# A graph attention loop whose first six steps of rows are gathered in the preparation, with later gathers of the first round not held back

## The chip, the cores and the metric

The kernel runs on one core of a Trainium2 chip. The metric is the device time of one execution in microseconds (us). The engines are named as in the profile: PE (matmul) and PEld (its weight load), DVE, ACT, POOL and SP. POOL issues the indirect DMAs ("gathers"), SP issues the ordinary ones.

## The reference, cut to what matters

One layer has three parts: a GATv2 graph attention, a four-layer linear-attention mixer over all 3125 nodes, and a mixture of eight experts. The change touches the first part only. There the graph has 3125 nodes with 256 features, 100,000 edges sorted by destination, and 4 heads of 64.

```python
x_l = (x @ W_l.T + b_l).reshape(n, HEADS, DIMS)
x_r = (x @ W_r.T + b_r).reshape(n, HEADS, DIMS)
...
s = x_l[src] + x_r[dst] + e_feat
s = jax.nn.leaky_relu(s, NEG_SLOPE)
alpha = jnp.einsum('ehc,hc->eh', s, att)
...
alpha = ex / (denom[dst] + 1e-16)
out = jax.ops.segment_sum(alpha[..., None] * x_l[src], dst, num_segments=n)
```

`x_l[src]` is the gather: each edge needs the row of its source node.

## The kernel before

The graph attention runs in three blocks, one after the other, and all engines meet at the end of each: the preparation (normalise, the products with W_l and W_r, index tables), the edge loop, and a closing block. Then come the mixer and the experts.

**Tiles and steps.** Edges are cut in items of 128 (TE). A step takes four items (IG), so it needs four gathers of 128 rows with 264 numbers each (GD) out of `xl_d`, the array of left products in the chip's main memory. There are 210 steps, in 15 rounds of 14 (RING). Round 0 is written out, rounds 1 to 14 are a loop (`rounds`, L1350 on), and its head is pinned to a fixed slot of a fetch block (`head_slot`), so that code ahead of it does not shift its body. The rows of a step lie in one of 14 places: the first six in `zone` (called XS in the profile), which in the preparation held x, the other eight in `ring` (called a_g).

**A step.** For step t of a round:

- SP loads, two steps ahead, the local destinations `DB` (a_db, L1399), and four steps ahead the edge attributes (a_lt, L1403). At step 5 it also stores two staged arrays of 448 KB each (L1433, L1434).
- DVE makes the one-hot matrix of the next step (L1642), then takes leaky relu times attention in two halves (`gate`, L1652), then sums per head (L1731). One L1731 ends each step of scores.
- PE computes the scores of items 0 and 1 (L1505, and L1506 that adds the gathered rows), counted by the semaphore a_scored0; then those of items 2 and 3 (L1512), counted by a_scored1, for which ACT has copied the gathered rows into PSUM (L1596).
- Ten to twelve steps later ACT weighs the rows (L1614), PE sums them (L1519) and DVE adds them up (L1659). From t = 7 of round 0 there is also a running maximum over batches of seven steps, the "chain".

PE's instructions for a step stand in the order first scores, chain, second scores, sums, and each engine runs its own list in order.

**Who waits for the rows.** The semaphore a_g of step t counts 16 for each gather that has landed. POOL issues the gathers of a step when the scores of three steps before are done (AHEAD = 3): it waits for a_scored0 ahead of the first of the four and for a_scored1 ahead of the third. Before step 2 of each round, POOL also gathers two staged arrays (L1471). In round 0 the first four steps (EARLY = 4) are an exception. The preparation gathers their 16 x 128 rows into `zone` (L1086), POOL waits for all of them at the end of the preparation (semaphore g_early), and the readers on PE (L1528) and ACT (L1593) do not wait in the loop.

**The end of the preparation.** DVE compares neighbouring edges' keys (L1284 to L1292), SP stores the result, two times 448 KB (L994), and a last small array (L996), and waits for these to land. Then the engines meet.

Of the kernel before, what the change touches and what calls it, by code (L numbers as in the profile page):

```python
# [36 lines left out]
IG = 4  # L37
# [11 lines left out]
RI = IG * RING  # L49
STAGED = RI * (ROUNDS + 2)  # L50
ZSLOTS = NT * D // (IG * GD)
EARLY = 4
LTS = BSTEPS
EA0 = GD
MW = EA0 + ED + 1
# [809 lines left out]
def graph_attention(nc, s, zone, XS, ident, x, xn_d, g, sums_d, scratch, ln1, ln1_of, scale0):  # L865
# [9 lines left out]
    with ExitStack() as keep:  # L875
# [4 lines left out]
        SRCX = kept("g_srcx", [TE, ITEMS], I32)  # L880
# [7 lines left out]
        with ExitStack() as c:  # L888
# [146 lines left out]
            def _(p):  # L1035
# [48 lines left out]
                p.wait_ge(s["p_xl_d"], 16 * (NW // XW))  # L1084
                for n in range(IG * EARLY):
                    p.indirect_dma_start(out=zone[:, n * GD:(n + 1) * GD], out_offset=None, in_=xl_d,  # L1086
                                         in_offset=bass.IndirectOffsetOnAxis(ap=SRCX[:, n:n + 1], axis=0)).then_inc(s["g_early"], 16)
                p.wait_ge(s["g_early"], 16 * IG * EARLY)

            @block.tensor  # L1090
            def _(pe):
# [210 lines left out]
        with ExitStack() as mid:  # L1302
# [3 lines left out]
            with ExitStack() as c:  # L1306
# [64 lines left out]
                def at_start(i):  # L1371

                    return isinstance(i, int) and i == 0

                def rows_landed(i, t):

                    return 64 * i if t < EARLY else 64 * i + 64

                def chain_of(i, t):

# [80 lines left out]
                def _(p):  # L1461
# [3 lines left out]
                    def slot(i, base, t):  # L1465
                        if t == GATHER_AT:
                            p.wait_ge(s["s_tiles"], 16 * i + 16)
                            wait(p, "s_staged", 32 * i, 0)
                            p.sem_inc(s["a_seen"], 1)
                            for n, a in enumerate((g["eaT"], g["ea"])):  # L1470
                                p.indirect_dma_start(out=STG[:, n, :], out_offset=None, in_=a,  # L1471
                                                     in_offset=bass.IndirectOffsetOnAxis(ap=TIX[:, 0:1], axis=0)).then_inc(s["s_gathered"], 16)
                        if t % BSTEPS == 0:
                            p.wait_ge(s[f"a_ix{t // BSTEPS}"], 16 * i + 16)
                            p.sem_inc(s["a_seen"], 1)
                        if at_start(i) and t < EARLY:
                            return
                        wait(p, "b_weighed", base, t + 1 - RING)
                        p.sem_inc(s["a_seen"], 1)
                        for j in range(IG):  # L1480
                            n = IG * (t % BSTEPS) + j
                            if j % 2 == 0:
                                wait(p, f"a_scored{j // 2}", base, t + 1 - AHEAD)
                                p.sem_inc(s["a_seen"], 1)
                            p.indirect_dma_start(out=gathered(t)[:, j, :], out_offset=None, in_=xl_d,  # L1485
                                                 in_offset=bass.IndirectOffsetOnAxis(ap=IX[:, t // BSTEPS, n:n + 1], axis=0)).then_inc(s[f"a_g{t}"], 16)
# [4 lines left out]
                def _(pe):  # L1491
                    def slot(i, base, t):
# [29 lines left out]
                        if scoring:  # L1522
# [2 lines left out]
                            ws = [pe.snap(both & 31).with_bounds(min_val=0, max_val=NW - 1), pe.snap(both >> 5).with_bounds(min_val=0, max_val=NW - 1)]  # L1525
                            wait(pe, "a_onehot", base, t + 1)
                            pe.wait_ge(s[f"a_eat{t % LTS}"], 32 * i + 16 * (t // LTS) + 16)
                            if not (at_start(i) and t < EARLY):  # L1528
                                pe.wait_ge(s[f"a_g{t}"], rows_landed(i, t))
                            scores_of_first(ws)  # L1530

                        if tau == 0:
# [55 lines left out]
                def _(a):  # L1588
                    def slot(i, base, t):
                        tau, odd, n = chain_of(i, t)  # L1590
                        par = 1 if odd else 0
                        if exists(base, t, 0):
                            if not (at_start(i) and t < EARLY):  # L1593
                                a.wait_ge(s[f"a_g{t}"], rows_landed(i, t))
                            wait(a, "a_gated1", base, t)
                            a.activation(pS[0:TE, 2:4, 0:GD], gathered(t)[:, 2:4, :], ACT.Copy).then_inc(s["a_filled"], 1)  # L1596
                        if tau == 3:
# [1010 lines left out]
```

## Time and profile before

| | us |
|---|---|
| median of 3 runs | 3437.3 |
| lowest, highest run | 3428.2, 3441.15 |
| the profiled execution | 3411.32 |
| its span (first to last instruction) | 3409.5 |
| mean granted TensorE clock | 0.953 |

The span is what the trace covers; about 2 us lie around it. The page gives busy times over the whole span: PE 3021.3 us (89%), DVE 1829.7 (54%), ACT 1508.7 (44%), POOL 1195.2 (35%). In the trace the preparation ends and the edge loop's block begins between 108 and 109 us. The edge loop ends at about 1543 us. The rest is the closing block, the mixer and the experts. A share over the whole says little of round 0, which lies between 109 and about 190 us. For that the timeline rows below are read.

### The profile page before, as it was taken

How to read it: one execution, taken by the hardware profiler on the slowest of the kernel's cores; microseconds unless marked ns; L12 is line 12 of the kernel's file. 1: busy time of each engine (PE TensorE's matmuls, PEld its weight loads, DVE VectorE, ACT ScalarE, POOL GpSimd, SP SyncE). 2: the span in 40 equal slices, each digit the busy share in tenths (PEclk: the TensorE clock that was granted, in tenths of full speed). 3: DMA queues.
4: the chain of work that ended last, by engine and by line, in shares of the span. 5: the costliest groups of instructions: out<-in, count | busy, mean ns of one | idle time of the engine just before them, and what ended most of it. 6: DMA issues, size and time to landing. Idle time of an engine off the chain costs nothing. (4 is left out here: it accounts for less than half of the span.)

```text
span 3409.5 us, 50817 instructions
## 1 busy us (share of the span) xinstructions
PE 3021.3 (89%) x13612; PEld 2391.3 (70%) x13613; DVE 1829.7 (54%) x3640; ACT 1508.7 (44%) x4942; POOL 1195.2 (35%) x1153
## 2 busy tenths in 40 slices
PE   6688888888888888884999999999999999999999
PEld 4456566556665556653778877877777888888898
DVE  5566676677666666676854464374455435111103
ACT  2067677677667667675422322232231222222232
POOL 4565565665656656530320041030012000222210
PEclk9798898999899998997999999999999999999999
DMA  7566665665666656543211011000001014333361
GB/s 216 151 152 146 149 143 141 150 150 144 149 148 149 148 146 144 143 97 116 63 38 37 27 31 31 27 22 1 15 27 50 1 39 162 120 120 120 121 173 41
DMA packets 288782, 345.06 MB, mean 101 GB/s; under 512 B 155205, under 2 KB 213684, under 8 KB 284666
## 3 DMA queue, kind: packets, MB, share of 16 engines
q1 hardware_dynamic: 232813, 174.79, 19.4%
q0 software_dynamic: 53632, 157.89, 18.0%
q10 hardware_dynamic: 2218, 10.81, 1.0%
q8 instruction: 74, 1.21, 0.2%
q14 instruction: 45, 0.37, 0.0%
HBM read 298.03 MB, written 44.37 MB: 100 GB/s over the span
## 5 line engine op out<-in xcount | busy, mean ns | idle before, releaser
L1485 POOL DMA_INDIRECT a_g<-xl_d,a_ix x480 | 475.0, 990 | 285.5 <-issue 124.5
L1519 PE MATMUL b_pM<-b_m,b_oh 128*112 128x281 f32 x1680 | 501.5, 443 | 44.5 <-DVE g_acc L1659 38.1
L1614 ACT ACTIVATE b_m<-a_g,c_pcx 128x64 f32<-128x64 f32 x1856 | 457.3, 333 | 13.1 <-issue 13.1
L1519 PEld LDWEIGHTS b_pM<-b_m,b_oh 128*112 128x112 f32 x1680 | 317.5, 195 | 174.9 <-issue 90.9
L1485 POOL DMA_INDIRECT XS<-xl_d,a_ix x344 | 337.0, 980 | 208.7 <-issue 92.5
L1652 DVE SCALAR_TENSOR_TENSOR a_r<-a_pS,g_attx 128x528 f32<-128x528 f32 x420 | 287.4, 700 | 192.2 <-remote 109.4
L1614 ACT ACTIVATE b_m<-XS,c_pcx 128x64 f32<-128x64 f32 x1424 | 349.3, 333 | 3.2 <-issue 3.2
L2306 ACT ACTIVATE f_hid<-f_pH,f_b 128x256 f32<-128x256 f32 (+3 forms) x360 | 162.0, 452 | 424.7 <-PE f_pH L2189 415.6
L449 PE MATMUL m_pH<-m_h,m_w 128*128 128x313 f32 (+1 forms) x1280 | 342.3, 426 | 4.5 <-DVE m_h L629 4.5
L125 POOL TENSOR_TENSOR m_rstd<-m_ve,m_mhalf 125x5 f32<-125x5 f32 x40 | 46.9, 1172 | 769.3 <-DVE m_ve L111 769.3
L449 PEld LDWEIGHTS m_pH<-m_h,m_w 128*128 128x128 f32 x1280 | 241.3, 189 | 97.2 <-issue 5.3
L1505 PE MATMUL a_pS<-g_xr,a_lt 128*128 x840 | 278.0, 414 | 20.7 <-issue 14.6
L1512 PE MATMUL a_pS<-g_xr,a_lt 128*128 x840 | 236.4, 405 | 65.0 <-ACT a_pS L1596 28.0
L2211 PE MATMUL f_pO<-f_w,f_hid 128*128 (+1 forms) x1296 | 287.3, 379 | 1.3 <-DVE XS L2443 1.3
L605 ACT ACTIVATE m_hid<-m_pH,m_b 128x313 f32<-128x313 f32 x320 | 149.5, 519 | 276.4 <-PE m_pH L449 276.4
L2211 PEld LDWEIGHTS f_pO<-f_w,f_hid 128*128 128x128 f32 (+1 forms) x1296 | 242.4, 189 | 34.2 <-ACT f_hid L2306 1.7
L1731 DVE TENSOR_REDUCE a_alpha<-a_r 128x16 f32<-128x1056 f32 x210 | 260.9, 1243 | 0.3
L1659 DVE TENSOR_TENSOR g_acc<-g_acc,b_pM 112x281 f32 x420 | 184.1, 438 | 87.7 <-remote 63.5
L1512 PEld LDWEIGHTS a_pS<-g_xr,a_lt 128*128 128x128 f32 x840 | 155.4, 195 | 107.4 <-issue 83.9
L1505 PEld LDWEIGHTS a_pS<-g_xr,a_lt 128*128 128x128 f32 x840 | 158.7, 200 | 72.5 <-issue 45.0
L426 PE MATMUL m_pO<-m_w,m_hid 128*125 128x256 f32 x896 | 202.6, 379 | 0.0
L376 PE MATMUL m_pH<-wide_w,turned 128*125 128x256 f32 x800 | 181.0, 382 | 9.4 <-ACT m_hid L555 9.4
(429 smaller groups left out, 4594.2 us busy)
## 6 DMA issues: line engine op xcount, KB each, us to landing
a_db<-dl_d SPq DMA_DIRECT2D x212, 224.0 KB
f_w<-in_ffn_W1p SPq DMA_DIRECT2D x16, 1024.0 KB
wide_w<-in_ffn_W1p SPq DMA_DIRECT2D x16, 1024.0 KB
m_w<-in_mix_W SPq DMA_DIRECT2D x8, 1024.0 KB
f_w<-in_ffn_W2p SPq DMA_DIRECT2D x8, 1024.0 KB
a_g<-xl_d,a_ix POOLq DMA_INDIRECT x480
a_lt<-eat_d SPq DMA_DIRECT2D x214, 32.0 KB
eat_d<-a_stage SPq DMA_DIRECT2D x15, 448.0 KB
```

What stands on the lines that cost most here:

```text
L376: ins = pe.matmul(pH[0:P, ROWS_OF(u), 0:D], HT[:, k, cols(g, j)], wqkv[:, k, (1 - n) * D:(2 - n) * D], start=(k == 0), stop=(k == KC - 1))
L426: ins = pe.matmul(o, lhs(k, j), rhs[:, k, :], start=(k == 0), stop=(k == chunks - 1))
L449: ins = pe.matmul(pH[:, b + h, 0:n], w1[:, k, f * 128:(f + 1) * 128], H2[:, k, at:at + n], start=(k == 0), stop=(k == KC - 1))
L1485: p.indirect_dma_start(out=gathered(t)[:, j, :], out_offset=None, in_=xl_d, in_offset=bass.IndirectOffsetOnAxis(ap=IX[:, t // BSTEPS, n:n ...
L1505: pe.matmul(o, lt[:, j, :], window_rows(0, ws), start=True, stop=False)
L1512: ins = pe.matmul(pS[0:TE, j, 0:GD], lt[:, j, :], window_rows(1, ws), start=False, stop=True, skip_group_check=True)
L1519: ins = pe.matmul(pM[0:WN, h, 0:MW], OH[:, b, j, :], M[:, b, j, :], start=(j == 2 * h), stop=(j == 2 * h + 1))
L1614: ins = a.activation(m[:, j, part], gathered(ts)[:, j, part], ACT.Copy, scale=of[:, first + j, h, 0:1])
L1652: v.scalar_tensor_tensor(out=R[:, 2 * h:2 * h + 2, :], in0=pS[0:TE, 2 * h:2 * h + 2, 0:GD], scalar=0.0, in1=attx[:, :].unsqueeze(1).broadc ...
L1659: v.tensor_tensor(w, w, pM[0:WN, h, 0:MW], ALU.add).then_inc(s[f"b_added{h}"], 1)
L1731: v.tensor_reduce(AX_[:, t // BSTEPS, :, i0:i0 + IG].rearrange("p h i -> p i h"), R[:, :, :].rearrange("p i (h d) -> p i h d", h=GH), AX.X ...
L2211: ins = pe.matmul(pO[0:m, j, 0:D], HID[:, hid, f, j * m:(j + 1) * m], second(f), start=(f == 0), stop=(f == FC - 1))
```

## The change

The preparation now gathers six steps instead of four (24 gathers), which is all that `zone` holds. Each gather raises the semaphore a_g of its own step, and POOL does not wait for them at the end of the preparation. The readers on PE and ACT wait for a_g in all steps of round 0. In the loop POOL begins with step 6, and up to step 9 (UNPACED = 10) it issues round 0's gathers with no wait for scores. The numbers that later rounds wait for in steps 0 to 3 rise by 64, since the first filling now counts too.

```diff
--- before.py
+++ after.py
@@ -49,7 +49,8 @@
 RI = IG * RING
 STAGED = RI * (ROUNDS + 2)
 ZSLOTS = NT * D // (IG * GD)
-EARLY = 4
+EARLY = 6
+UNPACED = 10
 LTS = BSTEPS
 EA0 = GD
 MW = EA0 + ED + 1
@@ -1084,8 +1085,7 @@
                 p.wait_ge(s["p_xl_d"], 16 * (NW // XW))
                 for n in range(IG * EARLY):
                     p.indirect_dma_start(out=zone[:, n * GD:(n + 1) * GD], out_offset=None, in_=xl_d,
-                                         in_offset=bass.IndirectOffsetOnAxis(ap=SRCX[:, n:n + 1], axis=0)).then_inc(s["g_early"], 16)
-                p.wait_ge(s["g_early"], 16 * IG * EARLY)
+                                         in_offset=bass.IndirectOffsetOnAxis(ap=SRCX[:, n:n + 1], axis=0)).then_inc(s[f"a_g{n // IG}"], 16)
 
             @block.tensor
             def _(pe):
@@ -1374,7 +1374,7 @@
 
                 def rows_landed(i, t):
 
-                    return 64 * i if t < EARLY else 64 * i + 64
+                    return 64 * i + 64
 
                 def chain_of(i, t):
 
@@ -1479,7 +1479,7 @@
                         p.sem_inc(s["a_seen"], 1)
                         for j in range(IG):
                             n = IG * (t % BSTEPS) + j
-                            if j % 2 == 0:
+                            if j % 2 == 0 and not (at_start(i) and t < UNPACED):
                                 wait(p, f"a_scored{j // 2}", base, t + 1 - AHEAD)
                                 p.sem_inc(s["a_seen"], 1)
                             p.indirect_dma_start(out=gathered(t)[:, j, :], out_offset=None, in_=xl_d,
@@ -1525,8 +1525,7 @@
                             ws = [pe.snap(both & 31).with_bounds(min_val=0, max_val=NW - 1), pe.snap(both >> 5).with_bounds(min_val=0, max_val=NW - 1)]
                             wait(pe, "a_onehot", base, t + 1)
                             pe.wait_ge(s[f"a_eat{t % LTS}"], 32 * i + 16 * (t // LTS) + 16)
-                            if not (at_start(i) and t < EARLY):
-                                pe.wait_ge(s[f"a_g{t}"], rows_landed(i, t))
+                            pe.wait_ge(s[f"a_g{t}"], rows_landed(i, t))
                             scores_of_first(ws)
 
                         if tau == 0:
@@ -1590,8 +1589,7 @@
                         tau, odd, n = chain_of(i, t)
                         par = 1 if odd else 0
                         if exists(base, t, 0):
-                            if not (at_start(i) and t < EARLY):
-                                a.wait_ge(s[f"a_g{t}"], rows_landed(i, t))
+                            a.wait_ge(s[f"a_g{t}"], rows_landed(i, t))
                             wait(a, "a_gated1", base, t)
                             a.activation(pS[0:TE, 2:4, 0:GD], gathered(t)[:, 2:4, :], ACT.Copy).then_inc(s["a_filled"], 1)
                         if tau == 3:
```

On POOL, in the preparation's end and the start of the edge loop, before (XS is `zone`, a_g is `ring`; a_scored0 and a_scored1 are the two counts of scores):

```order
L1086 DMA XS<-xl_d,g_srcx 128x264 x15
L888 UNCONDITIONAL_BRANCH [waits g_early]
...
L1471 DMA a_stage<-in_gnn_ea,a_tix 56x2048
L1485 DMA XS<-xl_d,a_ix 128x264 [waits a_scored0]
L1485 DMA XS<-xl_d,a_ix 128x264
L1485 DMA XS<-xl_d,a_ix 128x264 [waits a_scored1]
L1485 DMA XS<-xl_d,a_ix 128x264
...
L1485 DMA a_g<-xl_d,a_ix 128x264 [waits a_scored0]
```

The same place after the change:

```order
L1087 DMA XS<-xl_d,g_srcx 128x264 x23
L889 UNCONDITIONAL_BRANCH
...
L1471 DMA a_stage<-in_gnn_ea,a_tix 56x2048
L1485 DMA a_g<-xl_d,a_ix 128x264 x4
L1485 DMA a_g<-xl_d,a_ix 128x264 [waits a_ix1]
L1485 DMA a_g<-xl_d,a_ix 128x264 x11
L1485 DMA a_g<-xl_d,a_ix 128x264 [waits a_scored0]
```

Eight gathers (steps 4 and 5) moved from the loop into the preparation, and the next 16 (steps 6 to 9) stand without a wait for scores; the only one left among them is a_ix1, the index table of the second batch.

On ACT, the copies of gathered rows for steps 0 to 5 of round 0, before (a_gated1: DVE has read the place that is written):

```order
L1596 ACTIVATE a_pS<-XS 128x2x264 [waits a_opened]
L1596 ACTIVATE a_pS<-XS 128x2x264 [waits a_gated1] x3
L1596 ACTIVATE a_pS<-XS 128x2x264 [waits a_gated1,a_g4]
L1596 ACTIVATE a_pS<-XS 128x2x264 [waits a_gated1,a_g5]
```

And after:

```order
L1594 ACTIVATE a_pS<-XS 128x2x264 [waits a_g0,a_opened]
L1594 ACTIVATE a_pS<-XS 128x2x264 [waits a_gated1,a_g1]
L1594 ACTIVATE a_pS<-XS 128x2x264 [waits a_gated1,a_g2]
L1594 ACTIVATE a_pS<-XS 128x2x264 [waits a_gated1,a_g3]
L1594 ACTIVATE a_pS<-XS 128x2x264 [waits a_gated1,a_g4]
L1594 ACTIVATE a_pS<-XS 128x2x264 [waits a_gated1,a_g5]
```

Nothing moved here; four waits were added. PE's first scores of steps 0 to 3 get the same four.

## Rows read from the trace of the kernel before

**Rows 1.** The page: whole span, then queue rows (packets, MB, share).

```profile
span 3409.5 us, 50817 instructions
...
q8 instruction: 74, 1.21, 0.2%
```

**Rows 2.** Windows: stretch, length, busy us (instructions) per engine, PEclk, DMA share, GB/s.

```profile
94.00:104.00 10.00, 8.02 (x24) 5.94 (x24) 6.66 (x14) 0.00 (x0) 0.00 (x0) 0.62 0.02 7
131.00:134.00 3.00, 2.77 (x12) 2.02 (x12) 2.51 (x4) 0.03 (x1) 2.22 (x3) 1.00 0.96 307
136.00:142.00 6.00, 3.28 (x8) 2.56 (x9) 1.39 (x3) 0.61 (x1) 4.78 (x5) 0.50 0.77 225
```

**Rows 3.** Timeline, DVE, L1731 of steps 2 to 6: start, us, name.

```profile
126.33 1.26 DVE L1731 TENSOR_REDUCE a_alpha<-a_r 128x16 f32<-128x1056 f32 x1
...
130.30 1.25 DVE L1731 TENSOR_REDUCE a_alpha<-a_r 128x16 f32<-128x1056 f32 x1
...
134.86 1.25 DVE L1731 TENSOR_REDUCE a_alpha<-a_r 128x16 f32<-128x1056 f32 x1
...
144.35 1.25 DVE L1731 TENSOR_REDUCE a_alpha<-a_r 128x16 f32<-128x1056 f32 x1
...
150.52 1.25 DVE L1731 TENSOR_REDUCE a_alpha<-a_r 128x16 f32<-128x1056 f32 x1
```

**Rows 4.** Timeline, DVE, L1652 and L1642 of steps 2 to 7.

```profile
124.98 1.31 DVE L1652 SCALAR_TENSOR_TENSOR a_r<-a_pS,g_attx 128x528 f32<-128x528 f32 x2
...
128.96 1.31 DVE L1652 SCALAR_TENSOR_TENSOR a_r<-a_pS,g_attx 128x528 f32<-128x528 f32 x2
...
132.98 0.71 DVE L1652 SCALAR_TENSOR_TENSOR a_r<-a_pS,g_attx 128x528 f32<-128x528 f32 x1
...
146.69 0.36 DVE L1642 TENSOR_SCALAR a_lt<-a_db,a_node 112x512 f32<-112x512 f32 x1
...
149.78 0.71 DVE L1652 SCALAR_TENSOR_TENSOR a_r<-a_pS,g_attx 128x528 f32<-128x528 f32 x1 [2.11 <-remote]
...
156.38 0.71 DVE L1652 SCALAR_TENSOR_TENSOR a_r<-a_pS,g_attx 128x528 f32<-128x528 f32 x1 [4.21 <-remote]
```

**Rows 5.** Timeline, PE, first scores of steps 3, 4 and 5.

```profile
126.03 0.71 PE L1505 MATMUL a_pS<-g_xr,a_lt 128*128 x2 [1.04 <-DVE a_lt L1642]
...
130.83 0.71 PE L1505 MATMUL a_pS<-g_xr,a_lt 128*128 x2 [1.87 <-issue]
...
138.72 1.24 PE L1505 MATMUL a_pS<-g_xr,a_lt 128*128 x2 [4.95 <-issue]
```

**Rows 6.** Timeline, POOL: preparation's last gather, stage, first and last of steps 4, 5.

```profile
92.07 0.94 POOL L1086 DMA_INDIRECT XS<-xl_d,g_srcx  x1 [0.30 <-issue]
...
108.85 0.14 POOL L1462 IOTA a_node<- 128x1 f32 x1 [15.83 <-POOLq L888]
...
117.11 0.92 POOL L1471 DMA_INDIRECT a_stage<-in_gnn_ea,a_tix  x1 [0.30 <-issue]
...
121.37 0.98 POOL L1485 DMA_INDIRECT XS<-xl_d,a_ix  x1 [3.34 <-PE a_pS L1506]
...
131.41 0.95 POOL L1485 DMA_INDIRECT XS<-xl_d,a_ix  x1 [0.30 <-issue]
```

**Rows 7.** Timeline, SP: last stores of the preparation; steps 5 to 7.

```profile
104.04 0.57 SPq L994 DMA_DIRECT2D breaks_d<-i_dst_f  x1
...
129.91 0.43 SPq L1433 DMA_DIRECT2D eat_d<-a_stage  x1
...
133.04 0.33 SPq L1399 DMA_DIRECT2D a_db<-dl_d  x1
```

**Rows 8.** Timeline, DVE, preparation: the same shape with and without gathers beside.

```profile
74.84 1.07 DVE L1277 TENSOR_TENSOR i_ok<-i_ok,i_dst_f 128x896 f32<-128x896 f32 x1
...
100.23 1.08 DVE L1284 TENSOR_TENSOR i_dst_f<-i_dst_f,i_ok 128x896 f32<-128x896 f32 x1
```

**Rows 9.** Waits of DVE, 140 to 1500 us: total, times, longest.

```profile
DVE c_state L1736 <- remote: 98.2, 17, 8.4
```

## Prediction

> **What bounds the kernel now.** I read the page first, then the windows, then the timeline of each engine between 109 and 160 us, since the change touches only the end of the preparation and round 0 of the edge loop. The profiled execution took 3411.3 us, its span is 3409.5 us [rows 1], and its 15 rounds from 109 to about 1543 us are written as one round and 14 passes of a loop. Only one round can gain. The first sight is therefore one of size: all that can be won or lost directly lies in a few steps.
>
> In round 0, what ends a step of scores is the reduction L1731 on DVE. Its starts give the pace [rows 3]: 126.33 and 130.30 are steps 2 and 3, 3.97 us apart, with no row missing and with DVE nearly always busy. Step 4 follows after 4.56, step 5 after 9.49, step 6 after 6.17 us. Step 5 is the hole. PE shows why. Its first scores start 1.05 us after DVE's L1652 of the step before (124.98 to 126.03 for step 3), but 1.87 us after it for step 4 (128.96 to 130.83) and 5.74 us after it for step 5 (132.98 to 138.72) [rows 4, 5]. PE is 0.82 and 4.69 us late. The page calls the idle time "issue", which names nobody, but the rows of step 5 are what is missing. POOL began the loop's gathers only at 121.37, when scores released it, and the last of the eight, step 5's, is issued from 131.41 to 132.36 [rows 6], so PE starts 6.4 us after that issue ends. The DMA engines are 96% busy just then [rows 2], with SP's two stores of 448 KB from 129.91 on [rows 7] beside the gathers. POOL needs (131.41 - 121.37) / 7 = 1.43 us for a gather, so 5.7 us for a step's four, against a pace of 3.97: it can't catch up in steps 4 to 6.
>
> The wait has a second price. In 136 to 142 us the granted clock is 0.50, which is 1.2 GHz, after PE stood idle 4.95 us; in 131 to 134 it was 1.00, 2.4 GHz [rows 2, 5]. The scores of step 5 ran at the slower level. That is in the 9.49 us.
>
> **The change part by part.** *Steps 4 and 5 gathered in the preparation.* In the preparation POOL issues a gather in 0.94 + 0.30 = 1.25 us. The sixteenth starts at 92.07, the twenty-fourth will start at 92.07 + 8 x 1.25 = 102.1 and end at 103.0. POOL has nothing to do until 108.85, 15.83 us of idle time [rows 6], so this issue is covered; if the cover were gone it would cost 10 us. The transfers go into a stretch in which the DMA engines are 2% busy, 94 to 104 us [rows 2]. Only the last one or two can meet the stores that end the preparation, the second of which SP issues at 104.04 [rows 7]. A gather moves 128 x 264 x 4 bytes = 135 KB, 0.44 us at the 307 GB/s of rows 2, so the preparation's end moves by 0 to 0.9 us; I take 0.3, since most of the last gather's data is through before the second store starts. DVE's work there is not slowed: the same 128x896 shape took 1.07 us beside gathers (at 74.84) and 1.08 without (at 100.23) [rows 8]. Landing takes no more than the 6.4 us above: 109.4 for step 5's rows, needed at about 133.
>
> *The waits added in steps 0 to 3, and the one removed on POOL.* The rows of steps 0 to 3 are issued by 93.0 [rows 6], so the semaphores stand long before the loop. Behind PE's wait stand its second scores, behind ACT's the next copy, and neither waits longer. Nothing, bounds 0 and 0.3 us (one of POOL's own 0.30 us between instructions, the nearest row). The wait on g_early ended long before the engines met, and its end gives nothing.
>
> *The gain.* Steps 4 and 5 come at the pace of step 3: 4.56 - 3.97 = 0.59 and 9.49 - 3.97 = 5.52, in sum 6.1 us, the slow clock's part included. Steps 2 to 5 each carry the same clearing of a part of the accumulator on DVE, so the pace may be carried over.
>
> *Gathers of steps 6 to 9 not held back.* They start when POOL's stage gathers are issued, at 117.11 + 0.92 + 0.30 = 118.3 instead of 121.37 [rows 6]. Step 6's four end at 118.3 + 4 x 1.43 = 124.0, landed by 130.4, and PE wants them at about 133.4 + 4.0 = 137.4. Step 8's (twelve gathers) are there by 141.9 against 145.4, step 9's by 147.6 against 149.4 at the earliest. So rows are late in none of these steps. If they were still paced, step 7's would be released by the scores of step 4 near 132.9, and be there near 145, against 141.4. This part gives no gain of its own; it guards up to 3.6 us of the 6.1.
>
> *What is late next.* SP loads the destinations for step 7 at 133.04, behind the stores [rows 7]; DVE used them at 146.69 [rows 4], now at 146.69 - 6.1 = 140.6. That leaves 7.6 us, against the 6.4 us that a gather took in the same crowd: 0, at worst 1 us. After that come two idle times of DVE that end by "remote", 2.11 us before 149.78 (step 6) and 4.21 us before 156.38 (step 7) [rows 4]. Their matmuls seem to have ended before; the trace doesn't say what held them. I leave them as they are, because rows play no visible part, and keep as bounds that they vanish (-6.3) or grow by the same (+6.3).
>
> *After round 0.* Nothing in rounds 1 to 14 is timed from the start of the kernel, each step waits for a step before, and POOL is released by scores, so an early start is carried to the end in full.
>
> The sum: -6.1 + 0.3 + 0 + 0 = -5.8 us. Against the profiled execution that is 3411.3 - 5.8 = 3405.5. The median of the runs shown is 26 us above the profiled one, so for the median I subtract from it: 3437.3 - 5.8 = 3431.5, 0.17% less. A difference within 0.5% (17 us) can't be told from none in this kernel, whose own runs lie 13 us apart.
>
> **The rivals.**
> 1. *Another wait takes its place.* The late releases on DVE in steps 6 and 7 end at a time of their own, and step 6 waits until 149.78 as before. For it: both are unexplained, and SP and POOL have a share in the same crowd of transfers. Against it: after 156.38 every step would again have to be exactly as late. Gain 0, minus the 0.3: 3437.6.
> 2. *More goes than is counted.* Without the idle PE and its slower clock the two late releases vanish too: 5.8 + 2.1 + 4.2 = 12.1, 3425.2. For it: both follow the hole of step 5. Against it: such releases are found all over the loop, 98.2 us in 17 cases before L1736 alone [rows 9].
> 3. *Slower: the unheld gathers crowd out SP's loads.* Place: DVE's one-hot L1642 of steps 6 to 9, which needs SP's load of destinations. From 118.3 to 141 us there is always a gather in flight. A step's four rows took 7.3 us from the last issue's start (131.41 to 138.72) beside the stores, 5.2 for step 4 (125.7, that is 121.37 + 3 x 1.43, to 130.83). If each of four loads is later by twice this difference beyond its slack, 4 x 4.2 = 16.8 us are lost against 5.8 won: 3448.3. It decides from 1.5 us per step on. Against it: the loads are issued two steps ahead, some 7.6 us, and before the change gathers were in flight just as densely from 121.37 on.
> 4. *The loop's code lies elsewhere.* Each round has the late release of rows 9, 98.2 / 17 = 5.8 us. If it depended on where the body lies, 14 rounds could add or take a microsecond each: 3417 or 3445. The instruction queue's 74 packets are 1.21 MB, 16 KB each [rows 1]. The Trainium skill (Runtime: NRT & Kernel Launch, "Instruction fetch mechanics") has the engines refill their instructions in blocks of 16 KiB and pay for a taken branch out of the window; on the packet size the trace agrees, and by this rule code taken out ahead of a loop could move its cost. Against the rival stands that the kernel pins the loop's head to a slot of a fetch block.
>
> **How the numbers follow.** Forecast 56%, rival 1 17%, rival 2 13%, rival 3 8%, rival 4 6%, half of it to each side. Cases of both signs are within the spread of single runs (-9 to +4 us around the median), so I put this spread on each. The range from 3418 to 3447 leaves out the fast end of rivals 2 and 4 and the slow end of rivals 3 and 4. Faster by over 0.5% (under 3420.1) needs rival 2 or 4 and a low draw: 12%. Slower by over 0.5% (over 3454.5) needs rival 3 at its full price or 4: 6%. The rest is 82%.
>
> **What would show it right or wrong.** Right: 24 gathers in the preparation, the last starting near 102; the edge loop's first instructions near 109.1; PE's first scores of step 5 near 133.4 with no long idle time before them; L1731 of step 5 near 138; a granted clock of 1.00 from 136 to 142 us; POOL at step 6 from 118.3, and its first wait for scores before step 10; and round 1 and the end of the edge loop 5 to 6 us earlier. Wrong: step 5 early but step 8 not (rival 1), idle times of DVE before L1642 that end by a_db's landing (rival 3), rounds of another length than before (rival 4), or a PE that still idles 4 us before step 5, which would mean that the rows were not what it waited for.

## The result, and the profile after: slower by 9 us

The kernel after takes 3446.5 us in the median of 20 runs (3437.7 to 3459.7), the kernel before 3439.4 us beside it (20 runs, 3426.1 to 3451.2). The ratio is 1.0027, 95% interval 1.0015 to 1.0039, which is 9.3 us slower (5.2 to 13.4). I had forecast 5.8 us faster.

The two profiled executions lie further apart, 3444.2 against 3411.3 us. Three stretches tell why. The edge loop's block begins 9.35 us later (118.18 against 108.83). From there to the first reduction of round 1 it takes 95.1 us against 93.1, 2.0 more. From there to the loop's end it takes 1361.5 against 1341.0. This last 20.5 us is not the change: profiled one after the other on one chip, both kernels needed 1337 to 1338 us for it, so it belongs to the occasion. (On that same chip three other versions, profiled 28 minutes later, needed 1364 to 1368 us.) What the change did is the 9.35 and the 2.0.

**The preparation's end.** POOL's timeline of the kernel after (start, us, engine, line, operation; in brackets the idle time before it and what ended it), in answer to [rows 6]:

```profile
101.48 0.95 POOL L1087 DMA_INDIRECT XS<-xl_d,g_srcx  x1 [0.30 <-issue]
118.19 0.14 POOL L1462 IOTA a_node<- 128x1 f32 x1 [15.76 <-POOLq L889]
```

The last gather stands where I had put it, near 102, but POOL idles 15.76 us after it, as it did before the change (15.83). I had read that idle time as room. If it were room, it would have shrunk by the 9.4 us that the gathers now take. The preparation's end hangs on the last gather. DVE shows the chain; g_xr is the product with W_r, which PE computes into p_pP and DVE takes from there. First the kernel before:

```profile
91.25 0.43 DVE L1296 TENSOR_TENSOR g_xr<-p_pP,p_blr 112x264 f32<-112x264 f32 x1 [3.79 <-remote]
95.49 1.45 DVE L1296 TENSOR_TENSOR g_xr<-p_pP,p_blr 112x264 f32<-112x264 f32 x4 [3.81 <-remote]
98.12 0.43 DVE L1296 TENSOR_TENSOR g_xr<-p_pP,p_blr 112x264 f32<-112x264 f32 x1 [1.18 <-PE p_pP L1094]
```

and the same line after:

```profile
93.58 0.43 DVE L1296 TENSOR_TENSOR g_xr<-p_pP,p_blr 112x264 f32<-112x264 f32 x1 [3.81 <-remote]
102.05 0.43 DVE L1296 TENSOR_TENSOR g_xr<-p_pP,p_blr 112x264 f32<-112x264 f32 x1 [8.04 <-remote]
106.26 1.45 DVE L1296 TENSOR_TENSOR g_xr<-p_pP,p_blr 112x264 f32<-112x264 f32 x4 [3.77 <-remote]
```

In the second half of POOL's run of gathers DVE is let go once in 4 to 8.5 us. The last such release comes 3.8 us after the final gather (before: 93.01 to 95.49, 2.5 us), and the work that is left then takes the rest of the 15.8 us. PE says the same: it does its products four at a time while gathers are issued, and 20 in one stretch (24 in the kernel before) only after them:

```profile
102.54 2.10 PE L1094 MATMUL p_pP<-p_wlr,p_xt 128*112 128x264 f32 x4 [6.58 <-DVE g_xr L1296]
106.74 6.98 PE L1094 MATMUL p_pP<-p_wlr,p_xt 128*112 128x264 f32 x20 [2.11 <-DVE g_xr L1296]
```

**Round 0.** DVE after, the two halves of step 2 and then step 3, in answer to [rows 4]:

```profile
138.81 0.71 DVE L1650 SCALAR_TENSOR_TENSOR a_r<-a_pS,g_attx 128x528 f32<-128x528 f32 x1 [4.39 <-remote]
143.03 0.71 DVE L1650 SCALAR_TENSOR_TENSOR a_r<-a_pS,g_attx 128x528 f32<-128x528 f32 x1 [3.51 <-remote]
...
150.88 1.32 DVE L1650 SCALAR_TENSOR_TENSOR a_r<-a_pS,g_attx 128x528 f32<-128x528 f32 x2 [4.40 <-remote]
```

PE had done all of step 2's scores by 134.26, by these two rows (first scores' last products, second scores). DVE's two halves of step 2 were let go 5.4 and 8.8 us after them. That is what "late release" means below: the profile names no releaser ("remote"), and PE's work that DVE needs has ended.

```profile
132.77 0.61 PE L1506 MATMUL a_pS<-XS,ident 128*128 128x264 f32 x2
...
133.21 1.05 PE L1512 MATMUL a_pS<-g_xr,a_lt 128*128 x4
```

POOL meanwhile issued two stages and 16 gathers without a pause, from 125.05 to 148.56:

```profile
125.05 0.93 POOL L1471 DMA_INDIRECT a_stage<-in_gnn_eaT,a_tix  x1 [6.52 <-DMA a_tix<-tl_d]
...
147.61 0.95 POOL L1485 DMA_INDIRECT a_g<-xl_d,a_ix  x1 [0.31 <-issue]
```

Counted from the block's first instruction, the reductions of steps 1 to 7 begin before at 13.5, 17.5, 21.5, 26.0, 35.5, 41.7, 49.5 us, after at 13.5, 25.6, 34.1, 39.3, 43.3, 47.3, 51.1. Step 5's hole is gone: steps 4 to 7 take 17.0 us (34.1 to 51.1) instead of 28.0. But steps 2 and 3 lost 12.6. The granted clock, in answer to [rows 2] (stretch, length, busy us of PE, PEld, DVE, ACT and POOL, PEclk, DMA share, GB/s):

```profile
94.00:104.00 10.00, 3.35 (x8) 1.96 (x8) 0.45 (x2) 0.28 (x1) 6.60 (x7) 0.52 0.40 108
...
145.00:152.00 7.00, 1.80 (x5) 0.85 (x4) 2.42 (x5) 0.00 (x0) 2.94 (x3) 0.50 0.65 199
```

PE is at 1.2 GHz in 145 to 152, after 5.61 us of idle time ahead of step 3's first scores at 139.87. The slow stretch moved from step 5 to step 3. In 94 to 104 PE was busy 8.02 us before, 3.35 now.

### The profile page after: what moved, and what is told of

Read it like the earlier page. It is cut to its first block and busy times, and to the rows that moved or that the text cites. A ratio compares the mean times of both kernels' runs of the same rounds, so it can differ in the third digit from the quotient of the medians.

```text
span 3442.4 us, 50781 instructions
## 1 busy us (share of the span) xinstructions
PE 3038.8 (88%) x13612; PEld 2405.6 (70%) x13613; DVE 1830.4 (53%) x3640; ACT 1511.3 (44%) x4942; POOL 1188.8 (35%) x1153
## 5 line engine op out<-in xcount | busy, mean ns | idle before, releaser
L1519 PE MATMUL b_pM<-b_m,b_oh 128*112 128x281 f32 x1680 | 511.6, 450 | 33.3 <-DVE g_acc L1657 16.2
L1519 PEld LDWEIGHTS b_pM<-b_m,b_oh 128*112 128x112 f32 x1680 | 325.4, 199 | 162.2 <-issue 79.7
L1485 POOL DMA_INDIRECT XS<-xl_d,a_ix x336 | 326.2, 971 | 212.5 <-issue 88.2
L1505 PE MATMUL a_pS<-g_xr,a_lt 128*128 x840 | 279.1, 415 | 22.8 <-issue 12.6
```

Source lines behind the costliest of these rows:

```text
L1505: pe.matmul(o, lt[:, j, :], window_rows(0, ws), start=True, stop=False)
L1519: ins = pe.matmul(pM[0:WN, h, 0:MW], OH[:, b, j, :], M[:, b, j, :], start=(j == 2 * h), stop=(j == 2 * h + 1))
```

## The experiments

Two theories stood after the first result. **A**: an indirect DMA that POOL issues right behind another delays what DVE and ACT get from PE, so whatever is in progress beside a run of gathers stands nearly still until the run ends; the preparation pays for its eight further gathers in full. A has two forms: the issuing does it (A1), or the traffic of the rows (A2). **B**: the preparation's end is incidental, and the loss is the burst of unheld gathers in the loop.

The chips turned out to be of two kinds. On two of them (called quiet here) the kernel before takes 3151.7 and 3151.8 us, and no trace taken there has any wait of DVE or ACT that ends by "remote" in the preparation or the loop. On the others (called late) it takes 3411 to 3439 us; one late chip had it at 3411 and, 28 minutes later, at 3438, so that spread is not between chips. The mean granted clock differs too, 0.974 to 0.982 in the profiled executions of the quiet kind and 0.945 to 0.955 in the others; whether that is a cause or follows from PE's longer idle times is not shown. Each quiet chip was used on one occasion only, so that it is the chip and not the occasion is likely, not shown. Which kind a run got was not chosen. All results, times in us; "end" is the loop block's first instruction minus the first gather of the preparation; "round 0" runs from there to round 1's first reduction. A ratio is against the kernel before on the same chip.

| kernel | chip | gathers in the preparation | end | round 0 | ratio, interval |
|---|---|---|---|---|---|
| before (first profile) | late | 16 | 36.7 | 93.1 | |
| before_again | late | 16 | 36.6 | 92.7 | one run, 3408.8 |
| after (first profile) | late | 24 | 46.6 | 95.1 | 1.0027, 1.0015 to 1.0039 |
| after_again | late | 24 | 45.7 | 91.5 | 1.0002, 0.9984 to 1.0020 |
| prep6_held_3 | late | 24 | 46.9 | 90.7 | 1.0007, 0.9988 to 1.0025 |
| prep4_free10_3 | late | 16 | 35.8 | 99.0 | 1.0039, 1.0018 to 1.0060 |
| small24 | late | 24, small | 46.0 | 83.5 | one run, 3422.2 |
| act8_2 | late | 16, and 8 loads by ACT | 37.3 | 91.8 | one run, 3410.8 |
| poolbusy_2 | late | 16, then 8 memsets | 36.9 | 92.9 | one run, 3408.9 |
| loop8_held | late | 16, and 8 at the loop's start | 39.7 | 97.0 | 1.0009, 0.9993 to 1.0025 |
| two_two_2 | late | 8, and 8 at the loop's start | 26.1 | 95.7 | 0.9987, 0.9966 to 1.0007 |
| two_two_3 | late | 8, and 8 at the loop's start | 28.6 | 96.5 | 0.9995, 0.9977 to 1.0012 |
| prep6_held | quiet | 24 | 34.6 | 78.6 | 1.0019, 1.0006 to 1.0032 |
| prep4_free10 | quiet | 16 | 27.1 | 79.1 | 1.0002, 0.9982 to 1.0021 |
| prep4_free10_again | quiet | 16 | 28.4 | 79.5 | one run, 3147.4 |
| prep2_held | quiet | 8 | 27.7 | 93.0 | 1.0026, 1.0006 to 1.0047 |
| prep0_held | quiet | 0 | | 97.9 | 1.0045, 1.0029 to 1.0061 |
| act8 | quiet | 16, and 8 loads by ACT | 31.1 | 75.1 | one run, 3161.3 |
| poolbusy | quiet | 16, then 8 memsets | 33.4 | 83.6 | one run, 3145.8 |
| two_two | quiet | 8, and 8 at the loop's start | 26.3 | 83.1 | 0.9992, 0.9975 to 1.0010 |

Where the table says one run, the time serves for nothing: 29 runs of the kernel before on one late chip reach from 3429.2 to 3455.4 us. Such rows serve for their traces.

**The halves of the change, and fewer gathers in the preparation.** All with the change's other edits in place; "held" means that POOL waits for scores in round 0 as before.

```diff
-EARLY = 6
-UNPACED = 10
+EARLY, UNPACED = 6, 0    # prep6_held
+EARLY, UNPACED = 4, 10   # prep4_free10
+EARLY, UNPACED = 2, 0    # prep2_held
+EARLY, UNPACED = 0, 0    # prep0_held
```

> The changed kernel, but with round 0's gathers from step 6 on held back by scores as before (UNPACED = 0). Theory A (gathers issued one after another hold up what PE releases, wherever they stand): the preparation still ends about 9.4 us late (near 118 us instead of 108.8), because its last gather ends near 102.4 and the end followed that by 15.8 us in both traces; round 0 of the loop no more than 6 us shorter than before's; total 3 to 9 us slower than the kernel before. Theory B (the loop's free burst of 16 gathers is the loss, the preparation's end is chance): preparation ends near 109, total 3 to 6 us faster.

> Four steps gathered in the preparation as before, and the gathers of steps 4 to 9 free of scores. Theory A: preparation ends at 108.8 as before; in the loop 24 gathers run in one burst from 118 to about 149 us and steps 1 to 4 get late, about 12 us each way as in the changed kernel; total 0 to 4 us slower than before. Theory B: preparation as before, the whole loss of 7 to 9 us of the changed kernel is seen here.

> Two steps gathered in the preparation (8 gathers, 72 to 82 us), the rest in the loop and held back by scores. Theory A: the preparation ends about 10 us earlier (near 99 us, last gather's end plus 15.8, if nothing else bounds it first); the loop loses most of it again, since the rows of steps 2 and 3 come only after the two stage gathers (about 8 us late). Total within 4 us of before. Theory B: preparation ends near 109 as before and the loop loses 8 us.

> No gather in the preparation. It shows where the preparation ends without them. Theory A: near 95 us (its own work on PE and DVE without late releases), so 13 us earlier than before, and the loop starts with an empty store of rows and loses 8 to 14 us. Theory B: near 107 us, and the whole kernel some 10 us slower.

They ran on a quiet chip. prep6_held is slower by 6.0 us (1.9 to 10.1) without any burst of the change's in the loop, which B can't explain. Its POOL and DVE at the preparation's end:

```profile
95.54 0.28 DVE L1299 COPY i_any_turned<-i_pN 14x128 f32<-14x128 f32 x1 [0.47 <-PE i_pN L1151]
...
104.54 0.07 DVE L1624 MEMSET b_m<- 128x8 f32 x1 [8.72 <-PEq L889]
```

```profile
99.77 0.95 POOL L1087 DMA_INDIRECT XS<-xl_d,g_srcx  x1 [0.30 <-issue]
104.48 0.14 POOL L1462 IOTA a_node<- 128x1 f32 x1 [3.76 <-POOLq L889]
```

Here DVE is done at 95.8, nothing was held up, and it is POOL itself that everybody waits for: 24 gathers at 1.25 to 1.65 us are simply longer than the rest of the preparation. With 16 gathers POOL idles 6.01 us before the end, with 8 the end comes no earlier (27.7 against 27.1 and 28.4). So even where nothing is delayed the cover for eight more gathers did not exist; it cost 34.6 - 27.7 = 6.9 us (27.7 being also the mean of the two traces with 16). prep2_held and prep0_held lose in the loop instead, which waits for its rows: step 2's reduction begins 24.0 and 32.7 us after the block's first instruction, against 17.4 with 16 gathers. prep4_free10's burst costs nothing on this chip:

```profile
119.11 1.25 DVE L1729 TENSOR_REDUCE a_alpha<-a_r 128x16 f32<-128x1056 f32 x1
...
123.08 1.25 DVE L1729 TENSOR_REDUCE a_alpha<-a_r 128x16 f32<-128x1056 f32 x1
...
127.05 1.25 DVE L1729 TENSOR_REDUCE a_alpha<-a_r 128x16 f32<-128x1056 f32 x1
```

The pace is 3.97 us beside 26 indirect DMAs in a row. This is the pace that I had forecast.

**Both kernels again, and the preparation's gathers made small.** small24 is the kernel after with the preparation's 24 gathers cut from 264 numbers a row to 8, with as many rows each; the rows of steps 0 to 5 are then not the reference's.

```diff
-p.indirect_dma_start(out=zone[:, n * GD:(n + 1) * GD], out_offset=None, in_=xl_d,
+p.indirect_dma_start(out=zone[:, n * GD:n * GD + 8], out_offset=None, in_=xl_d.rearrange("n (a c) -> (n a) c", c=8),
```

> The kernel before, unchanged, for its trace on the chip of these runs. If releases by PE come late only on some chips, then: on a chip where the kernel takes about 3150 us no idle time of DVE ended by 'remote' in the edge loop, a preparation that ends near 98 us and a loop of about 1180 us; on a chip where it takes about 3440 us some 330 us of such idle time in the loop and a preparation that ends near 109 us, 15.8 us after the last gather.

> The changed kernel, unchanged. On a chip of the 3150 us kind: the preparation ends 3.7 us after POOL's last gather (near 104.5 us, 6.7 us later than with 16 gathers), since POOL's issue has become the last to end; the loop's first round saves 0 to 6 us; total 2 to 8 us slower than before. On a chip of the 3440 us kind: as measured, 9 us slower.

> The changed kernel with the 24 gathers of the preparation cut to 8 numbers a row instead of 264 (the same number of descriptors, 3% of the bytes; the rows of steps 0 to 5 are then not the reference's). An added fill of the zone moves everything by a few us, so times are counted from the first gather. Theory A1 (issue on POOL is what holds PE's releases up, or what ends last): the preparation ends as late after the first gather as with full rows, within 1 us. Theory A2 (the bytes in flight do it): it ends 6 to 9 us earlier.

The two kernels repeat their preparations within 1 us (36.6 and 45.7), but not the time: it shows 0.7 us between them (-5.5 to +6.8), where I had expected the 9 us again and the two traces have 7.9. small24 decides A1 against A2, as far as A2 means bytes:

```profile
95.49 0.43 DVE L1296 TENSOR_TENSOR g_xr<-p_pP,p_blr 112x264 f32<-112x264 f32 x1 [5.17 <-remote]
104.61 0.43 DVE L1296 TENSOR_TENSOR g_xr<-p_pP,p_blr 112x264 f32<-112x264 f32 x1 [8.69 <-remote]
```

With a 33rd of the bytes the releases are as late, and the end is at 46.0. A gather of 4 KB takes POOL as long as one of 135 KB:

```profile
94.55 0.95 POOL L1087 DMA_INDIRECT XS<-xl_d,g_srcx  x1 [0.30 <-issue]
95.80 0.95 POOL L1087 DMA_INDIRECT XS<-xl_d,g_srcx  x1 [0.30 <-issue]
```

small24 has as many rows to gather, so it can't tell POOL's writing of descriptors (the entries that say which row goes where) from the row transfers' number.

The Trainium skill (Perfetto Trace Analysis, "DMA Instruction — SWDGE (GPSIMD)") has the profiler's end of such a row at the last descriptor written and not at the data's landing; by that rule a row's time goes with its descriptors and not its bytes, and the trace agrees, 0.95 us for both sizes. small24's round 0 of 83.5 us is 7 us or more under every other one of a late chip. I have no explanation for it, and it is one trace.

**Steps 4 and 5 gathered at the start of the loop's block.** Four steps in the preparation, eight gathers on POOL ahead of all its other work in the block, the rest held.

```diff
+for n in range(IG * EARLY, IG * STRAIGHT):   # 4, 6
+    p.indirect_dma_start(out=zone[:, n * GD:(n + 1) * GD], out_offset=None, in_=xl_d,
+                         in_offset=bass.IndirectOffsetOnAxis(ap=SRCX[:, n:n + 1], axis=0)).then_inc(s[f"a_g{n // IG}"], 16)
```

> Sixteen gathers in the preparation as before; the eight of steps 4 and 5 are issued at the very start of the edge loop's block, in POOL's idle time of 7 us before its stage gathers, with no wait; from step 6 on held back by scores as before. On a chip of the 3150 us kind: preparation as before (near 98), loop's first round shorter by 0 to 6 us, total 0 to 6 us faster. On a chip of the 3440 us kind the burst of ten gathers from 109 to 121 us holds up the first two steps by some 4 us and step 5 gains 5: total within 4 us of before.

The end is at 39.7, 3 us over that of before, which A doesn't account for, and round 0 is 97.0 against 92.9. Step 1's reduction begins 15.6 us into the block instead of 13.5, step 3's 25.7 instead of 21.5: the eight gathers now hold up steps 0 to 3 in place of the preparation. Ratio 1.0009, no gain. Wherever these eight stood on a late chip, something paid.

**Is it POOL's work, or the indirect DMA?** act8 replaces the last eight gathers of the preparation by plain loads of as many bytes issued by ACT (the rows of steps 4 and 5 are then other nodes'). poolbusy keeps 16 gathers and the loop of before and adds eight memsets on POOL.

```diff
+for n in range(IG * EARLY, IG * STRAIGHT):   # act8: 4, 6, on ACT
+    a.dma_start(zone[:, n * GD:(n + 1) * GD], xl_d[128 * n:128 * n + 128, :]).then_inc(s["i_straight"], 16)
```

```diff
+for n in range(8):                           # poolbusy, on POOL
+    p.memset(spin[:, :], 0.0).then_inc(s["i_spun"], 1)
+    p.wait_ge(s["i_spun"], n + 1)
```

> The changed kernel with the last eight gathers of the preparation replaced by eight direct loads of the same 135 KB each from ACT's queue (rows of steps 4 and 5 are then other nodes' rows). Theory A (POOL's issuing holds PE's releases up): the preparation ends as with sixteen gathers, 36.6 us after POOL's first gather on a chip with late releases. Theory A2 (traffic in flight): it ends 45 to 46 us after it, as with 24.

> Sixteen gathers in the preparation, then POOL clears a tile of its own eight times (about 1 us each, no DMA); the loop held back by scores as before. If any work on POOL held up the releases, or POOL's end of work alone set the end of the preparation, it would end 45 us after the first gather as with 24 gathers. If it is the issuing of indirect DMAs, it ends 36 to 38 us after it.

> Four steps gathered in the preparation, gathers of steps 4 to 9 free of scores, once more for its trace: on a chip with late releases the burst of 24 gathers from 118 to 149 us makes steps 1 to 4 late by some 12 us and gives it back in steps 5 to 8, so that round 1 starts within 3 us of before's 92.7 to 93.1 us after the block's start.

> Eight gathers in the preparation (steps 0 and 1), the eight of steps 2 and 3 at the very start of the edge loop's block, in POOL's idle time, from step 4 on held back by scores as before. If the count of gathers issued one after another in the preparation is what moves its end: on a chip with late releases (about 3410 to 3440 us) the preparation ends 8 to 10 us earlier than before's (near 98 us), the rows of steps 2 and 3 arrive in time, and the total is 4 to 9 us less than before; on a chip without (about 3150 us) the preparation ends near 97 us as with sixteen, and the total is within 4 us of before. Rival (the end of the preparation has its own time): no gain on either.

These four fell on a quiet chip, where A has nothing to show, and left the question open. There eight memsets behind 16 gathers also move the end, from 27.1 and 28.4 to 33.4, since POOL then ends last, as in prep6_held. poolbusy also gave the loop of before on a quiet chip (round 0 83.6, step 5 after 9.8 us; prep6_held: 78.6 and 4.0). On a late chip:

> Eight of the preparation's 24 gathers replaced by direct loads of the same size from ACT's queue, once more. On a chip with late releases theory A (POOL's issuing of gathers holds PE's releases up) has the preparation end 36 to 38 us after the first gather, theory A2 (traffic in flight) 45 to 46 us. On a chip without: 31 us, as measured.

> Sixteen gathers, then eight clearings of a tile on POOL, once more. On a chip with late releases: 36 to 38 us after the first gather if only the issuing of indirect DMAs holds releases up, 45 us if any work on POOL does. On a chip without: 33 us, as measured.

> Steps 0 and 1 gathered in the preparation, steps 2 and 3 at the start of the edge loop's block, once more. On a chip with late releases: preparation ends 8 to 10 us earlier than before's 36.6 us after the first gather (so 26 to 29 us after it), rows of steps 2 and 3 in time or at most 5 us late, total 4 to 9 us less than before. On a chip without: again within 4 us of before.

poolbusy_2's POOL and DVE:

```profile
93.80 8.04 POOL L1091 MEMSET i_spin<- 128x1024 f32 x8
109.91 0.14 POOL L1466 IOTA a_node<- 128x1 f32 x1 [8.07 <-POOLq L889]
```

```profile
92.11 0.43 DVE L1300 TENSOR_TENSOR g_xr<-p_pP,p_blr 112x264 f32<-112x264 f32 x1 [3.82 <-remote]
96.36 1.45 DVE L1300 TENSOR_TENSOR g_xr<-p_pP,p_blr 112x264 f32<-112x264 f32 x4 [3.82 <-remote]
98.98 0.43 DVE L1300 TENSOR_TENSOR g_xr<-p_pP,p_blr 112x264 f32<-112x264 f32 x1 [1.18 <-PE p_pP L1098]
```

POOL is busy until 101.84, but DVE is let go for good at 96.36, 2.6 us after the last gather's end, and the preparation ends 16.1 us after that gather. The memsets cost nothing: 36.9. In act8_2 the same bytes come by ACT's queue, issued in 3.73 us:

```profile
92.14 3.73 ACTq L1038 DMA_DIRECT2D XS<-xl_d  x8
```

and the end is at 37.3. (These loads start 2.8 us after the last gather's end, beside PE's and DVE's remaining work.) So on a late chip 8 more indirect DMAs cost 9 to 10 us, 8 small ones as much, 8 plain loads of the same size or 8 other POOL instructions at most 0.7. With 8 gathers fewer (two_two) the end comes 8 to 10.6 us earlier, and the same DVE line runs without a late release both beside the eight and behind them:

```profile
78.46 0.43 DVE L1297 TENSOR_TENSOR g_xr<-p_pP,p_blr 112x264 f32<-112x264 f32 x1 [0.37 <-PE p_pP L1095]
...
82.45 0.43 DVE L1297 TENSOR_TENSOR g_xr<-p_pP,p_blr 112x264 f32<-112x264 f32 x1 [0.57 <-PE p_pP L1095]
...
85.45 0.43 DVE L1297 TENSOR_TENSOR g_xr<-p_pP,p_blr 112x264 f32<-112x264 f32 x1 [0.44 <-PE p_pP L1095]
86.45 0.43 DVE L1297 TENSOR_TENSOR g_xr<-p_pP,p_blr 112x264 f32<-112x264 f32 x1 [0.57 <-PE p_pP L1095]
87.45 0.43 DVE L1297 TENSOR_TENSOR g_xr<-p_pP,p_blr 112x264 f32<-112x264 f32 x1 [0.57 <-PE p_pP L1095]
```

(two_two_3, whose gathers of the preparation run from 72.22 to 83.03.) This limits A. The first eight gathers of the preparation cost next to nothing: with only them a late chip ends it at 26.1 and 28.6, a quiet one at 26.3. In all 12 traces of late chips DVE has no wait over 1.8 us beside these eight, in nine of them none over 0.6 us. DVE's waits of 3 to 9 us all end 12 us or more after the first gather, from the tenth gather on. So the price is not an even one per gather: next to nothing for the first eight, 8 to 10.6 us for the second and 9 to 10 us for the third.

two_two_2 and two_two_3 gain at the end and lose 2.8 and 3.6 us in round 0. I had expected a time 4 to 9 and 4 to 8 us less; it shows 4.4 less (11.6 less to 2.4 more) and 1.7 less (7.9 less to 4.1 more), so no gain is shown.

**The two halves on a late chip, and two_two once more.** The halves had been seen on a quiet chip only.

> The preparation's half of the change alone: six steps of rows gathered there, the loop's gathers held back by scores as before. Where the preparation ends by the last gather's end plus some 15.8 us (as in before and after on the chips that take about 3410 us): theory A (back-to-back gathers on POOL hold up releases of PE) expects the loop's block 45 to 46 us after the first gather instead of 36.6, +9 us, less the 5 to 6 us that steps 4 and 5 come earlier at pace: +2 to +5 us in the time. Theory B (the loss is the unheld burst in the loop): block at most 38 us after the first gather and 5 us faster than before. Where there are no late releases (about 3150 us): block 34.6 us after the first gather, ratio 1.002 again.

> The loop's half of the change alone: four steps gathered in the preparation as before, steps 4 to 9 with no wait for scores. On a chip of about 3410 us, theory A: block 36.6 us after the first gather as before; round 0 (block to the end of its fourteenth step) 91 to 96 us against 92.7, so within 3 us of before, ratio 0.999 to 1.001, with late releases of DVE during the burst. Theory B: round 0 at least 6 us longer, ratio over 1.0015. On a chip of about 3150 us: as before, ratio 1.000.

> Two steps gathered in the preparation, steps 2 and 3 at the start of the loop's block, the rest held as before, for a narrower interval. Theory A, on a chip of about 3410 us: block 26 us after the first gather against 36.6, round 0 some 3 us longer, in sum -4 to -8 us, ratio 0.9977 to 0.9988. A theory by which only the loop's steps count: +3 us, ratio 1.001.

The preparation's half: end 46.9 (+10), round 0 90.7 (-2.2 against the mean 92.9 of three loops like that of before), as A expects in kind; I had expected 5 to 6 us back in round 0. Step 5's reduction begins 29.7 us into the block instead of 35.5 to 36.2, but step 7's at 48.0 instead of 49.5 to 50.6: two late releases in step 7 (waits of 2.85 and 3.53 us) take back most of what step 5 gained. The time says +2.4 us (-4.1 to +8.6). The loop's half: end 35.8, round 0 99.0, +6.1, which I had expected within 3 us; the time says +13.4 us (6.2 to 20.6). B had 6 us or more here, so B was right on the burst and A's sizing of it wrong. B was wrong that the preparation's end is incidental (46.9), and what holds the burst's steps up is A's late releases. DVE in this burst of 26 indirect DMAs, to be held against the even pace of the same kernel on the quiet chip above:

```profile
137.84 0.71 DVE L1650 SCALAR_TENSOR_TENSOR a_r<-a_pS,g_attx 128x528 f32<-128x528 f32 x1 [2.35 <-remote]
139.93 0.71 DVE L1650 SCALAR_TENSOR_TENSOR a_r<-a_pS,g_attx 128x528 f32<-128x528 f32 x1 [1.39 <-remote]
...
151.34 1.38 DVE L1650 SCALAR_TENSOR_TENSOR a_r<-a_pS,g_attx 128x528 f32<-128x528 f32 x2 [7.96 <-remote]
```

The last release of the burst comes 2.1 us after its last gather's end (149.21). So neither half is a gain on a late chip. In the whole change the loop's burst is shorter (18) and its cost is about what the prepared rows give back.

Whether this runs through the whole loop can be counted. In three traces of late chips (before_again, after, prep4_free10_3), from 200 to 1500 us, DVE and ACT have 463 idle times over 0.5 us that end by "remote". Runs of back-to-back gathers fill 75% of that time, and the 2.5 us behind each run a further 22%. About 400 of the 463 (86%) end in those 2.5 us, the others inside a run, none later. That they gather behind a run's end, where less than a quarter of the time lies, is what A says, but it doesn't show the direction. In the loop POOL itself waits for PE's scores, so a release that is late for any reason would also end POOL's run and let POOL and DVE go together; in before_again 30 of DVE's 43 waits over 0.5 us that end by PE lie behind a run too. The direction rests on the runs in which POOL waits for nothing: the preparation, and the bursts.

## Why the prediction was wrong, point by point

**The step that failed** is the first of the parts: "POOL has nothing to do until 108.85, 15.83 us of idle time [rows 6], so this issue is covered; if the cover were gone it would cost 10 us". The term stood at +0.3 (0 to 0.9) and measured +9.35 in the first pair of traces, +9.1 in the second. The idle time was not free time: it was as long because the engines had to catch up on what the gathers had held back, so it moved along with them. The 10 us that I named for a missing cover were the right number. I had tested whether DVE's instructions beside gathers get longer (1.07 against 1.08 us, [rows 8]) and they don't; I had not looked at the idle time between them, which had "remote" in it at 91.25 and 95.49. On a quiet chip the term fails too, for a plainer reason: the cover left by 16 gathers is 6.01 us and not 15.83, and eight more cost 6.9.

**The gain of 6.1 us in steps 4 and 5** was right in mechanism and nearly in size: on a quiet chip step 5 goes from 9.8 to 4.0 us and round 0 from 83.6 to 78.6, 5.0 us. On late chips the held version keeps 2.2 of it. The prediction left DVE's waits in steps 6 and 7 at 6.3 us; in prep6_held_3 they are 8.9 us, and step 7 keeps 1.5 to 2.6 us of the gain.

**The unheld gathers, costed at nothing and as a guard of 3.6 us**, are nothing on a quiet chip, and on a late one delay steps 2 and 3 by 12.6 us, of which steps 4 to 7 give back 11.0. Without the prepared rows the burst costs 6.1.

**"What is late next"**: I left the two "remote" waits of steps 6 and 7 as they were, "because rows play no visible part". The rows don't, their gathers do. This is the same miss as the first: with 98.2 us in 17 such waits before one line [rows 9], the kind of wait was known to be dear, and its cause was what the change moved.

**The waits added for steps 0 to 3** cost nothing that can be seen: step 1 follows step 0 after 3.0 us as before. SP's loads of destinations did not come into play either.

**The rivals.** Rival 3 named the right sign, and 3448.3 is near the 3446.5 measured, but its place (DVE's one-hot behind SP's loads) was wrong: no idle time before that line ends by a load in steps 2 to 9. It was right by accident. Rival 1 was right in that another wait took the place (prep6_held_3, step 7), but it had no loss. Rivals 2 and 4 fell; rounds 1 to 14 were as long in both kernels when profiled on one chip (1338.0 and 1336.7 us).

**The range and the resolution.** The measured 3446.5 lies just inside my 3418 to 3447, but only because the spread of single runs was put on it; the sign was wrong, and the range is no credit to the mechanism. I had also held a difference under 17 us to be beyond telling; the median of 20 runs told 9.3 us to within 4.1.

**What stays open.** What inside the chip passes a release late while POOL issues indirect DMAs, and why two chips don't show it: no run here tells. Nor is the split exact. The two pairs of traces have +11.4 and +7.9 us for the whole change, its two timings +9.3 and +0.7, with 4 and 6 us to each side. Its halves alone are timed at +2.4 (preparation) and +13.4 us (loop), with 6 and 7 us to each side, and need not add. Open too is why the first eight gathers of the preparation hold up next to nothing, while in the loop, where a run has 5.6 gathers in the mean (before_again, 200 to 1500 us), releases are late all along. No version beat the kernel before: two_two, which has half the gathers in the preparation, lies at 0.9992, 0.9987 and 0.9995, each interval holding 1.

## What to carry to other kernels

An engine's idle time covers added work only if it shrinks when work is added. Look at when it ends relative to the engine's last instruction, and whether others were held up in the meantime; if the stretch always ends a fixed time after that engine's work, it is a chain and not a gap. Idle times that end by "remote" need a cause before a change that moves DMA issues is costed: list which other engine's runs they line up with. And a tuned kernel should be timed on more than one chip, since here the same code differs by 8 to 9% and the price of an edit by its whole size.

## What the runs showed of the hardware that was not expected

- On some chips, runs of indirect DMAs issued back to back by POOL go with idle times of DVE and ACT of 2 to 9 us that end by "remote" (in round 0, up to 8.8 us after PE's last row). 24 small ones do it as well as 24 large ones; the first eight in the preparation, plain loads from ACT's queue and POOL's memsets do not.
- The same kernel takes 3152 us on chips without these releases and 3411 to 3439 us on chips with them. The loop from round 1 on takes 1094 to 1108 us on the one kind and 1329 to 1368 us on the other, which is nearly the whole difference.
- An indirect DMA of 128 rows most often occupies POOL for 0.95 + 0.30 us, whatever the rows' length (32 bytes or 1056); in loop bursts single ones took up to 1.96 us.
